# Where TensorE spreads the next pair's delta*u: in front of a pair's expert step, or behind it

## The chip, the cores and the metric

One core of a Trainium2 chip. The metric is the device time of one execution in microseconds.

## The reference

A block of a state-space layer and a mixture of experts over the same 4096 normalised rows x of 256. Cut to what matters:

```python
xn = layernorm(x)
# branch 1: 128 channels d, 64 states n, a scan over the 4096 rows
h = exp(delta[d] * A[d, n]) * h + (delta[d] * u[d]) * B[n]      # each row in turn
y[d] = sum over n of h * C[n]
s = xn + ((y + u * D) * silu(right)) @ W_down
# branch 2: 8 experts, the best 2 for each row
hid = silu(xn @ w1[e]) * (xn @ w3[e]);  out += weight * (hid @ w2[e])
x + s * silu(out)
```

All values are float32.

## The kernel before

**The scan.** The rows are cut into eight chunks of 512. In a chunk the 128 channels form 64 pairs: a pair is two channels with 64 states each on 128 partitions, so there are 512 pairs s, each worked on as 128 x 512. For a pair

- TensorE *spreads* the two channels' delta*u over the states into a PSUM bank: one matmul with a matrix of zeros and ones, `spread(s)`, L1166. Two banks take turns, so a spread waits for the product two before it (L1165).
- VectorE multiplies the spread with B (the *product*, `mult(s)`, L914) and runs the scan (`scan(s)`, L924).
- ScalarE has made the decay, exp(delta * A), into a PSUM bank (L660), from delta that a DMA brought (L565).
- GpSimd multiplies the states by C (`state_by_c`, L420; in the first chunk VectorE does one in four, L960), and TensorE sums the products of four pairs over the states (`reduce_quad`, L1101).

From the second chunk on, every fourth pair (s % 4 == 3) has no spread: GpSimd makes its product from a DMA (L428). So there are 400 spreads.

**The experts.** The chosen rows are sorted by expert into tiles of 256, 39 at most, of which 35 are planned as live. A tile has a turn `rows` (transposes on TensorE, L1138, evicted by ScalarE, L587) and eight turns `step`. In a step TensorE first does the output product of the step three back, `expert_out` (L1123, it needs `hid` from GpSimd, L442), and then `gate_and_up` (L1154) into one of two PSUM banks. ScalarE takes tanh (L595) and a copy (L597) from it, VectorE the *gates* (L936), which frees the bank for the turn after next (`bank_free`, L1169). At a tile's end ScalarE evicts its output (L604). For a tile that is not live TensorE does tiny matmuls instead (L1090).

**The order.** `BY_PAIR` says which turns stand at which pair: steps from pair 64 on, somewhat less than one turn a pair up to pair 484, up to two from there. Among the turns are also the products for the next chunk (L1061) and, at the sixth and eighth pair of a chunk, the two *down* products of the chunk before (`down`, L1110). For these VectorE first closes the chunk in its fifth pair (L943, L945), and then adds each to the rows (`add_rows`, L952), which frees their bank. In pairs 11 to 36 of a chunk VectorE and ScalarE also prepare the next one (a convolution in three taps, L755 and L758; clip, L779). In pairs 0 to 12 of the first chunk TensorE has the up-projections (`left_right`, L1052) and transposes (L1014) of all chunks.

Each engine runs its own queue in the order written. VectorE's, for each pair, cut to what matters here:

```python
            for s in range(PAIR_COUNT):
                if not on_pool(s):
                    mult(s)
                ...
                if s:
                    scan(s - 1)
                    gates(BY_PAIR[s - 1])
                c, at = s // PAIRS, s % PAIRS
                if c and at == 5:
                    gate_chunk(c - 1)
                if c and at - 2 in DOWN_AT:
                    add_rows(c - 1, DOWN_AT[at - 2])
```

TensorE's is in the functions that follow.

Of the kernel before, what the change touches and what calls it, by code (L numbers as in the profile page):

```python
# [14 lines left out]
PAIR_COUNT = NC * PAIRS  # L15
# [67 lines left out]
def on_pool(s):  # L83

    return s >= PAIRS and s % 4 == 3
# [19 lines left out]
def states(s, on_vector):  # L105

    return sum(state_on_vector(i) == on_vector for i in range(s + 1))
# [14 lines left out]
def mamba_and_experts(nc, x, gam, bet, w_up, b_up, conv_w, conv_b, w_dl, b_dl, w_b2, w_c2, a_log,  # L122
                      dvec, w_dn, b_dn, gate, w_all, c_ident, c_upper, c_pick, c_win, c_first,
                      c_start, c_token, out):
    with ExitStack() as ctx:
# [145 lines left out]
        def ge(eng, s, n):  # L271

            if n > 0:
                eng.wait_ge(s, n)
# [733 lines left out]
        def _(pe):  # L1008
# [24 lines left out]
            def transpose_y(c):  # L1033

                pe.wait_ge(s_yh, c + 1)
                if c == 0:
                    pe.wait_ge(s_xev, NC)
                elif c == 1:
                    pe.wait_ge(s_rt, 1)
                else:  # L1040
                    pe.wait_ge(s_lrev, c)
                transpose_chunk(yh, (c % YH_RING) * TC, banks[0:2] if c == 0 else gu_bank).then_inc(s_ytr, 1)

            def left_right(c):

                pe.wait_ge(s_yev, c + 1)
                if c == 1:
                    pe.wait_ge(s_slot, 1)
                ge(pe, s_lrev, c)
                for m, bank in enumerate((banks[2], banks[3]) if c == 0 else (o_bank, gu_bank[0])):  # L1050
                    for h in range(2):
                        ins = pe.matmul(bank[:, :], wup[:, h, m * P:(m + 1) * P], colsT[c % 2][:, h, :],  # L1052
                                        start=(h == 0), stop=(h == 1))
                ins.then_inc(s_lr, 1)

            def product(c, kind):

                if kind == "delta":
                    pe.wait_ge(s_u, c + 1)
                w = wdl[:, :] if kind == "delta" else wbc[:, "bc".index(kind), :]  # L1060
                pe.matmul(product_bank(c, kind)[:, :], w, stage("u"), start=True, stop=True).then_inc(s_dp if kind == "delta" else s_bc, 1)  # L1061
# [30 lines left out]
            def reduce_quad(q):  # L1092

                i = q % QUADS
                pe.wait_ge(s_hc, states(4 * q + 3, False))
                ge(pe, s_hcv, states(4 * q + 3, True))
                if i == 0:
                    pe.wait_ge(s_bcev, 2)
                    ge(pe, s_gt2, q // QUADS)
                for g in range(4):  # L1100
                    ins = pe.matmul(y_bank[32 * g:32 * g + 32, :], win[:, 30 - 2 * i:62 - 2 * i],  # L1101
                                    p_ring[:, (4 * q + g) % P_RING, :], start=(i == 0), stop=(i == QUADS - 1),
                                    skip_group_check=True)
                ins.then_inc(s_red, 1)

            def down(c, h):

                pe.wait_ge(s_gated, c + 1)
                for n in range(2):
                    ins = pe.matmul(bank_of(("down", c, h))[:, n * D:(n + 1) * D], gated[:, (2 * h + n) * P:(2 * h + n + 1) * P],  # L1110
                                    wdn[:, :], start=True, stop=True)
                ins.then_inc(s_dn, 1)

            def expert_out(k):

                i, r = k // KS, k % KS
                pe.wait_ge(s_hid, k + 1)
                if r == 0:
                    ge(pe, s_oev, i)

                def products():
                    for s in range(SH):
                        ins = pe.matmul(o_bank[:, s * D:(s + 1) * D], hid[:, k % 4, s * P:(s + 1) * P],  # L1123
                                        wring[:, r, 4 * P:WROW], start=(r == 0 and s == 0), stop=(r == KS - 1),
                                        skip_group_check=True)
                    return ins

                if_live(i, products, o_bank, s_o)

            def transpose_rows(i):  # L1130

                bank = bank_of(("rows", i, 0))
                pe.wait_ge(s_xg, 32 * (i + 1))

                def products():
                    for h in range(2):
                        for s in range(SH):
                            ins = pe.transpose(bank[:, h * SLOT + s * P:h * SLOT + (s + 1) * P],  # L1138
                                               xg[:, s, h * P:(h + 1) * P], ident[:, :])
                    return ins  # L1140

                if_live(i, products, bank, s_tr)

            def gate_and_up(i, kk):

                bank = bank_of(("step", i, kk))
                if kk == 0:
                    pe.wait_ge(s_xgT, i + 1)
                pe.wait_ge(s_w[kk], 16 * (i + 1))

                def products():
                    for m in range(2):
                        for h in range(2):
                            ins = pe.matmul(bank[:, m * SLOT:(m + 1) * SLOT], wring[:, kk, (2 * m + h) * P:(2 * m + h + 1) * P],  # L1154
                                            xgT[:, i % 2, h, :], start=(h == 0), stop=(h == 1))
                    return ins

                if_live(i, products, bank, s_gu)

            def spread(s):  # L1160

                c, g, i16 = s // PAIRS, s % 4, (s % PAIRS) // 4
                if s % PAIRS == 0:
                    pe.wait_ge(s_stack[c % 2], 32 * (c // 2 + 1))
                ge(pe, s_bm, ORDER[s] - 1)  # L1165
                pe.matmul(du_bank[ORDER[s] % 2][:, :], pick[:, QUADS * (g % 2) + i16, :], stack[:, c % 2, g // 2, :],  # L1166
                          start=True, stop=True).then_inc(s_sel, 1)

            def bank_free(n):  # L1169

                if n < 2:
                    pe.wait_ge(s_lrev, NC)
                    return
                kind, t, k = TURNS[n - 2]
                if kind == "step":
                    pe.wait_ge(s_gt, KS * t + k + 1)
                elif kind == "rows":
                    pe.wait_ge(s_xgT, t + 1)
                elif kind == "down":
                    pe.wait_ge(s_add, 2 * t + k + 1)  # L1180
                elif kind == "delta":
                    pe.wait_ge(s_dlt, KD * t + 1)
                else:
                    pe.wait_ge(s_bcev, 2 * t + 1 + "bc".index(kind))

            def turns(here):

                for turn in here:
                    kind, t, k = turn
                    if kind == "step" and KS * t + k >= LAG:  # L1190
                        expert_out(KS * t + k - LAG)
                    bank_free(NUMBER[turn])
                    if kind == "rows":
                        transpose_rows(t)
                    elif kind == "step":
                        gate_and_up(t, k)
                    elif kind == "down":
                        down(t, k)
                    else:
                        product(t, kind)  # L1200

            spread(0)
            for s in range(PAIR_COUNT):
                if s + 1 < PAIR_COUNT and not on_pool(s + 1):
                    spread(s + 1)
                if s % 2 == 0 and s <= 2 * (NC - 2):
                    left_right(s // 2 + 1)
                if s % 2 == 1 and s <= 2 * (NC - 2) - 1:
                    transpose_y(s // 2 + 2)
                if s % 4 == 3 and s >= 7:  # L1210
                    reduce_quad((s - 7) // 4)
                turns(BY_PAIR[s])
            reduce_quad(PAIR_COUNT // 4 - 1)
            turns(BY_PAIR[PAIR_COUNT])
            for k in range(KS * TILES - LAG, KS * TILES):
# [41 lines left out]
```

## Time and profile before

| | |
|---|---|
| median of three runs | 1525.58 us (1524.34 to 1527.27) |
| the profiled execution's own time | 1526.07 us |
| its span, from the first to the last instruction | 1524.3 us |
| busy TensorE / VectorE / GpSimd / ScalarE | 1222.2 / 1222.3 / 1154.3 / 721.6 us |
| mean granted TensorE clock | 0.900 of full speed |

Three engines are busy for three quarters or four fifths of the span, so the busy times of the whole say little on the bound. The stages differ: set-up until the first scan at 103.5 us, the first chunk without experts up to some 266, the expert steps among the pairs up to 1376, the last pairs with the steps of tiles that are not live, and from 1458 the last sums and stores. Matmul ends in the profile are modelled.

### The profile page before, as it was taken

The numbers are of one execution on the slowest core, as the hardware profiler recorded it, in microseconds if no ns is written. First come the engines' busy times: TensorE is split into PE (matmuls) and PEld (weight loads), VectorE is DVE, ScalarE is ACT, GpSimd is POOL, SyncE is SP. The second block draws the span as 40 slices with busy tenths as digits, with TensorE's granted clock in tenths as the row PEclk, the third lists the DMA queues.
The fourth block names the chain that finished last, engine by engine and source line by source line (L and its number), as shares of the span: only waits on it lengthen the run. The fifth ranks groups of instructions, "written<-read, shape, count | busy, mean of one in ns | idle before, by whom it ended". The sixth has DMA issues, their size and how long they took to land. (4 is left out here: it accounts for less than half of the span.)

```text
span 1524.3 us, 21337 instructions
## 1 busy us (share of the span) xinstructions
PE 1222.2 (80%) x5496; PEld 860.7 (56%) x5496; DVE 1222.3 (80%) x1597; ACT 721.6 (47%) x1557; POOL 1154.3 (76%) x1088
## 2 busy tenths in 40 slices
PE   5737655889988999889989999889988999896720
PEld 5613111566756677556666677657756676674410
DVE  6545999888787978799888987898778988787738
ACT  1445533464544555354555555455535555455611
POOL 0233788779896888778987888789977788799953
PEclk9969655899999999999999999999999999997555
DMA  9843697556564557446655855646744684754336
GB/s 239 168 128 94 169 283 206 150 151 189 172 224 132 171 165 254 129 133 204 220 158 160 250 171 158 228 126 208 232 140 127 181 259 149 255 166 145 121 117 221
DMA packets 173124, 272.52 MB, mean 179 GB/s; under 512 B 28544, under 2 KB 70144, under 8 KB 172992
## 3 DMA queue, kind: packets, MB, share of 16 engines
q10 hardware_dynamic: 111072, 173.93, 39.3%
q1 hardware_dynamic: 55104, 78.41, 16.7%
q0 software_dynamic: 6816, 18.69, 3.2%
q8 instruction: 50, 0.82, 0.2%
q14 instruction: 82, 0.67, 0.1%
HBM read 225.20 MB, written 45.76 MB: 178 GB/s over the span
## 5 line engine op out<-in xcount | busy, mean ns | idle before, releaser
L420 POOL TENSOR_TENSOR arena<-arena,c_rep 128x512 f32<-128x512 f32 x498 | 595.5, 1202 | 183.9 <-DVE arena L924 177.8
L924 DVE TENSOR_TENSOR_SCAN arena<-bank,carry,arena 128x512 f32<-128x512 f32 x512 | 651.9, 1274 | 75.2 <-ACT bank L660 69.9
L1154 PE MATMUL bank<-xgT,wring 128*128 128x256 f32 x2240 | 534.1, 381 | 17.8 <-DVE xn L952 7.1
L660 ACT ACTIVATE bank<-arena,a_neg 128x512 f32<-128x512 f32 x512 | 354.7, 693 | 261.5 <-DVE arena L924 111.0
L1154 PEld LDWEIGHTS bank<-xgT,wring 128*128 128x128 f32 x2240 | 424.0, 190 | 87.7 <-DVE gt L936 13.8
L1123 PE MATMUL bank<-wring,hid 128*128 128x256 f32 x1120 | 301.3, 392 | 44.9 <-ACT o_sb L604 44.6
L914 DVE TENSOR_TENSOR arena<-bank,b_rep 128x512 f32<-128x512 f32 x400 | 272.3, 681 | 40.4 <-PE bank L1166 32.4
L1166 PE MATMUL bank<-stack,pick 128*128 128x512 f32 x400 | 234.7, 598 | 73.3 <-DVE arena L914 51.9
L595 ACT ACTIVATE th<-bank 128x256 f32<-128x256 f32 x312 | 118.9, 381 | 367.6 <-PE bank L1154 309.2
L1123 PEld LDWEIGHTS bank<-wring,hid 128*128 128x128 f32 x1120 | 205.8, 192 | 150.2 <-issue 101.9
L442 POOL TENSOR_TENSOR hid<-gt,ue 128x256 f32<-128x256 f32 x312 | 244.9, 786 | 38.3 <-DVE gt L936 34.9
L936 DVE SCALAR_TENSOR_TENSOR gt<-th,bank 128x256 f32<-128x256 f32 x312 | 126.3, 405 | 132.1 <-ACT th L595 65.9
L1166 PEld LDWEIGHTS bank<-stack,pick 128*128 128x128 f32 x400 | 83.3, 209 | 141.6 <-DVE arena L914 96.3
L1101 PE MATMUL bank<-arena,win 128*32 128x512 f32 x1024 | 157.2, 690 | 3.0 <-POOL arena L420 3.0
L428 POOL TENSOR_TENSOR arena<-arena,b_rep 128x512 f32<-128x512 f32 x112 | 142.6, 1273 | 0.1
L597 ACT ACTIVATE ue<-bank 128x256 f32<-128x256 f32 x312 | 117.7, 377 | 6.9 <-POOL hid L442 6.8
L448 POOL DMA_INDIRECT results<-o_sb,goal x78 | 78.1, 1001 | 26.1 <-issue 16.5
L410 POOL DMA_INDIRECT x_sorted<-xn,route x64 | 64.3, 1005 | 37.9 <-DVE xn L885 24.8
L1090 PEld LDWEIGHTS bank<-ident 128*128 128x128 f32 x136 | 31.0, 293 | 39.6 <-issue 38.1
L1090 PE MATMUL bank<-ident 128*128 128x2 f32 x136 | 30.9, 324 | 24.9 <-POOL hid L442 13.8
L1110 PE MATMUL bank<-wdn,tails 128*128 128x256 f32 x64 | 24.2, 519 | 31.3 <-DVE tails L945 20.6
L1101 PEld LDWEIGHTS bank<-arena,win 128*32 128x32 f32 x1024 | 21.2, 114 | 49.2 <-issue 36.2
(148 smaller groups left out, 744.9 us busy)
## 6 DMA issues: line engine op xcount, KB each, us to landing
arena<-delta_d ACTq DMA_DIRECT2D x512, 256.0 KB, 4.0
arena<-du_d ACTq DMA_DIRECT2D x112, 256.0 KB, 4.2
wring<-in_w_all SPq DMA_DIRECT2D x64, 384.0 KB, 5.5
x_sorted<-arena SPq DMA_DIRECT2D x2, 5031.0 KB, 38.5
xg<-x_sorted ACTq DMA_DIRECT2D x39, 256.0 KB
arena<-results SPq DMA_DIRECT2D x16, 512.0 KB, 6.3
xn<-in_x SPq DMA_DIRECT2D x4, 1024.0 KB, 9.5
parts_d<-spare SPq DMA_DIRECT2D x16, 256.0 KB, 4.2
```

The lines of the kernel that those rows point to most:

```text
L420: pool.tensor_tensor(p_ring[:, s % P_RING, :], h_ring[:, s % H_RING, :], of_chunk(c_rep, c, 2), ALU.mult).then_inc(s_hc, 1)
L428: pool.tensor_tensor(product_with_b(s), product_with_b(s), b_rep[:, cols(c)], ALU.mult).then_inc(s_bp, 1)
L442: pool.tensor_tensor(hid[:, k % 4, :], gt[:, k % 2, :], ue[:, k % 2, :], ALU.mult).then_inc(s_hid, 1)
L595: act.activation(th[:, :], bank[:, 0:SLOT], ACT.Tanh, scale=0.5).then_inc(s_th, 1)
L660: act.activation(a_bank[s % 2][:, :], dl_ring[:, s % D_RING, :], ACT.Exp, scale=a_neg[:, s % PAIRS:s % PAIRS + 1]).then_inc(s_exp, 1)
L914: v.tensor_tensor(product_with_b(s), du_bank[n % 2][:, :], b_rep[:, cols(c)], ALU.mult).then_inc(s_bm, 1)
L924: v.tensor_tensor_scan(out=h_ring[:, s % H_RING, :], data0=a_bank[s % 2][:, :], data1=product_with_b(s), initial=carry[:, q:q + 1], op0=AL ...
L936: v.scalar_tensor_tensor(out=gt[:, k % 2, :], in0=th[:, :], scalar=1.0, in1=bank_of((turn, i, kk))[:, 0:SLOT], op0=ALU.add, op1=ALU.mult). ...
L1101: ins = pe.matmul(y_bank[32 * g:32 * g + 32, :], win[:, 30 - 2 * i:62 - 2 * i], p_ring[:, (4 * q + g) % P_RING, :], start=(i == 0), stop=( ...
L1123: ins = pe.matmul(o_bank[:, s * D:(s + 1) * D], hid[:, k % 4, s * P:(s + 1) * P], wring[:, r, 4 * P:WROW], start=(r == 0 and s == 0), stop ...
L1154: ins = pe.matmul(bank[:, m * SLOT:(m + 1) * SLOT], wring[:, kk, (2 * m + h) * P:(2 * m + h + 1) * P], xgT[:, i % 2, h, :], start=(h == 0) ...
L1166: pe.matmul(du_bank[ORDER[s] % 2][:, :], pick[:, QUADS * (g % 2) + i16, :], stack[:, c % 2, g // 2, :], start=True, stop=True).then_inc(s_ ...
```

## The change

On TensorE the spread of pair s + 1 is issued behind the turns of pair s, not in front of all that pair s has. It also comes behind the up-projection, the transposes and the reduction that pair s may have. The first spread stays where it is.

```diff
             spread(0)
             for s in range(PAIR_COUNT):
-                if s + 1 < PAIR_COUNT and not on_pool(s + 1):
-                    spread(s + 1)
                 if s % 2 == 0 and s <= 2 * (NC - 2):
                     left_right(s // 2 + 1)
                 if s % 2 == 1 and s <= 2 * (NC - 2) - 1:
                     transpose_y(s // 2 + 2)
                 if s % 4 == 3 and s >= 7:
                     reduce_quad((s - 7) // 4)
                 turns(BY_PAIR[s])
+                if s + 1 < PAIR_COUNT and not on_pool(s + 1):
+                    spread(s + 1)
             reduce_quad(PAIR_COUNT // 4 - 1)
```

## Rows read from the trace of the kernel before

**Rows 1.** Busy us by stage: PE, PEld, DVE, ACT, POOL; PEclk, DMA, GB/s

```profile
158.00:266.00 108.00, 60.60 (x150) 16.92 (x149) 102.93 (x118) 41.18 (x71) 85.37 (x83) 0.56 0.82 227
266.00:1376.00 1110.00, 1006.41 (x4748) 736.95 (x4749) 928.09 (x1134) 563.37 (x1246) 925.73 (x883) 0.98 0.59 181
1376.00:1458.00 82.00, 54.15 (x224) 35.21 (x222) 57.32 (x82) 45.37 (x112) 76.08 (x77) 0.58 0.37 117
```

**Rows 2.** TensorE's waits, 270 to 1376 us: us in total, times, longest

```profile
PE bank L1123 <- ACT o_sb L604: 44.6, 33, 2.1
PE bank L1110 <- DVE tails L945: 19.0, 6, 4.2
PE bank L1110 <- DVE xn L952: 10.6, 6, 2.5
PE bank L1154 <- DVE xn L952: 7.1, 6, 1.8
PE bank L1061 <- DVE gt L936: 5.3, 3, 2.4
PE bank L1154 <- DVE spare L779: 4.2, 4, 2.1
PE bank L1154 <- DVE gt L936: 4.0, 6, 1.1
PE bank L1166 <- DVE arena L914: 3.3, 7, 0.8
```

**Rows 3.** VectorE's waits in the same stretch

```profile
DVE gt L936 <- ACT th L595: 65.3, 56, 4.0
...
DVE gt L936 <- ACT ue L597: 48.1, 35, 2.0
```

**Rows 4.** Timeline, pairs 135 to 137: start, length, engine, line, idle

```profile
457.75 1.89 PE L1154 MATMUL bank<-xgT,wring 128*128 128x256 f32 x8
...
459.29 0.58 PE L1166 MATMUL bank<-stack,pick 128*128 128x512 f32 x1
...
460.43 0.42 DVE L936 SCALAR_TENSOR_TENSOR gt<-th,bank 128x256 f32<-128x256 f32 x1 [3.65 <-ACT th L595]
...
461.50 1.13 PE L1110 MATMUL bank<-wdn,tails 128*128 128x256 f32 x4 [1.62 <-DVE xn L952]
...
462.28 0.58 PE L1166 MATMUL bank<-stack,pick 128*128 128x512 f32 x1
...
462.70 1.02 PE L1123 MATMUL bank<-wring,hid 128*128 128x256 f32 x4
```

**Rows 5.** Timeline of VectorE, 704 to 706 us

```profile
704.04 0.66 DVE L914 TENSOR_TENSOR arena<-bank,b_rep 128x512 f32<-128x512 f32 x1
704.63 1.27 DVE L924 TENSOR_TENSOR_SCAN arena<-bank,carry,arena 128x512 f32<-128x512 f32 x1
705.82 0.39 DVE L936 SCALAR_TENSOR_TENSOR gt<-th,bank 128x256 f32<-128x256 f32 x1
```

**Rows 6.** Timeline of VectorE, then of TensorE, at the start of chunk 6

```profile
1120.71 0.42 DVE L936 SCALAR_TENSOR_TENSOR gt<-th,bank 128x256 f32<-128x256 f32 x1 [0.61 <-POOL hid L442]
...
1124.31 2.04 PE L1110 MATMUL bank<-wdn,tails 128*128 128x256 f32 x4 [4.16 <-DVE tails L945]
```

**Rows 7.** Timeline of VectorE, pairs 13 and 14

```profile
152.94 0.69 DVE L914 TENSOR_TENSOR arena<-bank,b_rep 128x512 f32<-128x512 f32 x1
...
154.78 0.73 DVE L758 SCALAR_TENSOR_TENSOR spare<-c_rep,half,spare 128x512 f32<-128x512 f32 x1
156.98 0.69 DVE L914 TENSOR_TENSOR arena<-bank,b_rep 128x512 f32<-128x512 f32 x1 [1.48 <-PE bank L1166]
158.63 1.28 DVE L924 TENSOR_TENSOR_SCAN arena<-bank,carry,arena 128x512 f32<-128x512 f32 x1 [0.96 <-ACT bank L660]
```

**Rows 8.** Busy time in two short stretches, columns as in rows 1

```profile
800.00:803.00 3.00, 3.00 (x11) 2.42 (x10) 2.20 (x3) 0.00 (x0) 3.00 (x4) 0.63 0.57 200
1124.00:1130.00 6.00, 5.69 (x17) 2.91 (x18) 4.91 (x6) 0.69 (x1) 3.20 (x3) 0.51 0.30 101
```

## The prediction

> **What bounds the kernel now.** I read the busy times by stage first [rows 1]. From pair 15 to 62 VectorE is busy 102.93 of 108 us. In the stretch of the expert steps, 1110 us of the span of 1524.3, TensorE is busy 1006.41 us, 91%, against 928.09 on VectorE and 925.73 on GpSimd. In the one behind it, where the last pairs run with the steps of tiles that are not live, GpSimd is busy 76.08 of 82. So most of the time belongs to TensorE, and a change of its order is worth what it does to TensorE's 104 idle microseconds among the expert steps. The view of waits says what ends them [rows 2]: ScalarE's eviction of a tile's output (44.6 us, 33 times), VectorE's closing of a chunk and its two additions to the rows (19.0, 10.6 and 7.1 us, six times each), and gates and clips (5.3, 4.2 and 4.0 us, 13 times). The waits that the change takes aim at, a spread in front of a step that waits for a product on VectorE, come to 3.3 us there. Seen from VectorE, the gates waited for ScalarE's tanh or copy 56 and 35 times [rows 3], 91 of the 280 steps of live tiles: in a third of the steps VectorE is ahead of TensorE, in the others it is late on its own account.
>
> **The change part by part.** The same 400 spreads run, no DMA moves, and no wait is written that was not there. Only TensorE's queue changes; SP's, ScalarE's and GpSimd's keep their order. Between two steps there stands one spread as before, but it is that of the pair whose product VectorE needs next, no longer that of the pair after it.
>
> *What is late next.* VectorE's iteration s+1 is: product of s+1, scan of s, gates of the step of s, all in one queue. Before, the spread of s+1 was done before the step of s, so where VectorE was ahead only the gates were left when the step ended. Now product, scan and gates all stand behind the step. The price of this way from TensorE over VectorE follows from two timelines [rows 4, 5]. A step's gate-and-up matmuls begin at 457.75 and the spread behind them at 459.29: 1.54 us. The spread lasts 0.58, and the product needs it whole. From product to scan are 0.59 (704.04 to 704.63), from scan to gates 1.19 (to 705.82). That makes 1.54 + 0.58 + 0.59 + 1.19 = 3.90 us from the step's begin to its gates. Today it is 460.43 - 457.75 = 2.68. **Such a hop costs 1.22 us more** where VectorE was ahead; where its gates are already that late, it costs nothing.
>
> *Where a hop is paid.* With a step in every pair the gates' lateness is hidden: the step after next needs the bank that they free, and a whole step lies between. It is paid where TensorE today stands idle for VectorE. The gates of pair 135 [rows 4] run at 460.43, the addition to the rows follows, and TensorE, 1.62 us idle, begins the second down product at 461.50. At a chunk's start [rows 6] the gates at 1120.71 are followed by the two operations that close the chunk, and TensorE begins at 1124.31 after 4.16 us idle; what stands behind that down product waits with it, since TensorE keeps its order. These are the three sixes of the waits [rows 2]: the closing, the second down product, and the step that needs the second addition. 18 x 1.22 = 22.0 us. I take off two, for chunk starts at which VectorE is late anyway (a choice): 16 x 1.22 = **+19.5**. Bounds: half of the 18, 11.0, and all, 22.0.
>
> *The 13 waits for gates and clips* are of the same kind, but many lie where VectorE has extra work for the next chunk and is late already. Between 0 and 13 x 1.22 = 15.9 I take a third, **+5.3**, as a third of the gates wait for ScalarE [rows 3].
>
> *The first pairs.* For pairs 1 to 13 the spread now follows a chunk's up-projection or its transposes. The chain of these between TensorE and ScalarE does not wait for it, but VectorE does [rows 7]: the product of pair 13 runs at 152.94; VectorE is through with what follows it, the scan of 12 and a tap of the convolution, at 154.78 + 0.73 = 155.51, 2.57 us later. Behind the projection its spread takes the place that pair 14's has today, so it runs at 156.98, the product of 14 at 159.55 and the scan of 13 0.59 later, at 160.1, where it is at 158.63: **+1.5**. The stage behind it is VectorE's, which carries this on. In that stage almost no pair has a turn, and a spread waited for the product two pairs back in any case: the edit costs nothing, hidden behind VectorE's 95%; were VectorE not the bound there, its reductions would delay the spreads.
>
> *The last pairs.* The spread now stands behind steps that wait for GpSimd. GpSimd's 82 - 76 = 6 idle microseconds are little room. Bounds 0 and one hop for each of the seven groups of four pairs, 8.5; I take **+2**, near the lower end, as an engine that is nearly full hides what others lose.
>
> *The waits for the eviction* end a fixed time after a step, and a spread inside them is free. Every fourth pair has no spread; gone through in the order that the program writes out, 12 of the 33 waits gain one and two lose one. A spread takes at most 462.70 - 462.28 = 0.42 us [rows 4]. Between 0 and 10 x 0.42 = 4.2 I take half, **-2**.
>
> *The clock.* After the 4.16 us idle the granted clock is 0.51 over 6 us, that is, mostly 1.2 GHz, and 0.63 over 3 us after an addition's wait at pair 264 [rows 8], against a mean of 0.98 in the stretch [rows 1]. A fall costs at most 6 x 0.49 = 2.9 or 3 x 0.37 = 1.1 us; I take 2.0. The six waits before the second down product grow from 1.6 to 2.8 us. Between no fall and six, 12 us, I take three, **+6**. The Trainium skill, TensorE: Matmul & The Clock Gate, section "What's actually happening", has the low clock as the engine's default, which activity lifts, and lets it fall after an idle window of its own; read strictly, these six need not fill one, and by that the sum would be 6 us lower. The row at pair 264 speaks for falls.
>
> **Sum.** 19.5 + 5.3 + 1.5 + 2 - 2 + 6 = +32.3 us. The profiled execution took 1526.07 us (span 1524.3, the rest lies around it), so 1558.4; it stands 0.5 above the median of the three runs, which gives **1558 us**.
>
> **The rivals.**
> *A, no change:* VectorE is late at the 18 places anyway, so a hop costs nothing. For it: in two thirds of the steps the gates did not wait for ScalarE. Against: at such a place nothing but the step held them, VectorE had waited 3.65 us for tanh before 460.43 [rows 4]. What is left is 1.5 + 2 - 2, so 1527.
> *B, faster:* TensorE, the bound, loses the 3.3 us in front of the spreads and wins 4.2 at the evictions: 7.5 less, 1518. It decides if a hop costs under 7.5 / 18 = 0.4 us. For it: TensorE's 91%. Against: nothing in the chain [rows 4, 5] can be left out.
> *C, much slower:* all hops at full price, six falls, the last pairs at their upper end: 22.0 + 15.9 + 1.5 + 8.5 + 12 = 60, so 1586, and beyond if GpSimd, which gets its inputs 1.2 us later in a third of the steps, falls behind as well. For it: GpSimd is 83% busy. Against: its product is needed only three steps later.
>
> **How the numbers follow.** The forecast has 0.70, A 0.14, B 0.08, C 0.08. The forecast's own range goes from half of the 18 hops with the first pairs and all of the evictions' gain (11.0 + 1.5 - 4.2 = 8, so 1534) to 1586. A lies below it. To leave out no more than two tenths the range is 1530 to 1584. 0.2%, 3 us, is about what a measurement of this kernel can tell from no change: slower 0.78, same 0.14, faster 0.08.
>
> **What would show it.** In the changed profile VectorE's products wait for their spread in about as many pairs as the gates waited for ScalarE before, and the gates' 113 us of waiting nearly vanish. From a step's first matmul to its gates are 3.9 us where VectorE is ahead. TensorE's waits for the closing and the additions grow from 36.7 us towards 57 at the same counts, some with a lower clock behind them; those for the eviction stay near 45. The scan of pair 13 comes 1.5 us later, and the stage from there to pair 62 is as long as before. I am wrong if the gates do not move against their step, or if they move and those 18 waits do not grow: then the time there was not TensorE's.

## The result, and the profile after

The changed kernel takes **1594.01 us** (median of 4 runs, 1592.76 to 1595.03) against 1526.42 (1524.34 to 1528.68) for the kernel before on the same chip: a ratio of 1.0443, 95% interval 1.0422 to 1.0464, 4.4% slower. The forecast was 1558, in a range of 1530 to 1584: the direction was right, and the loss is 68 us where 32 were forecast.

The same three stages as [rows 1], each moved by what its beginning and its end fell back (the scans of pairs 62 and 484 come 2.1 and 52.0 us later):

```profile
160.10:268.10 108.00, 60.53 (x154) 16.89 (x150) 103.57 (x121) 41.04 (x70) 88.55 (x85) 0.57 0.77 229
268.00:1428.00 1160.00, 1018.42 (x4757) 744.08 (x4750) 925.20 (x1134) 565.49 (x1250) 929.22 (x883) 0.97 0.56 173
1428.00:1526.00 98.00, 55.87 (x214) 35.78 (x213) 57.68 (x82) 44.30 (x108) 76.28 (x77) 0.54 0.31 97
```

About 2 us are lost before pair 62, 50 among the expert steps and 16 in the last pairs; what follows is as long as before. VectorE and GpSimd do the same work in nearly the same busy time. TensorE in the second stage is busy 1018.42 us where [rows 1] has 1006.41, so 12.0 of the 50 are longer busy time for the same instructions, and its idle time rose from 103.6 to 141.6, by 38.0.

TensorE's waits in that stage, beside [rows 2]:

```profile
PE bank L1123 <- ACT o_sb L604: 42.2, 33, 2.0
PE bank L1110 <- DVE tails L945: 24.5, 6, 6.6
PE bank L1110 <- DVE xn L952: 19.6, 7, 2.9
PE bank L1154 <- DVE gt L936: 13.9, 20, 2.1
PE bank L1154 <- DVE xn L952: 12.5, 7, 2.0
PE bank L1154 <- DVE spare L779: 8.0, 5, 4.1
PE bank L1101 <- POOL arena L420: 7.9, 8, 2.6
PE bank L1123 <- POOL hid L442: 3.3, 3, 1.8
PE bank L1061 <- DVE gt L936: 2.6, 2, 2.0
PE bank L1138 <- DVE gt L936: 2.3, 4, 1.2
PE bank L1061 <- DVE spare L765: 2.1, 2, 1.5
```

The closing and the two additions (tails and twice xn) grew from 36.7 to 56.6 us. The waits for gates and for the convolution (gt and spare) went from 14.2 to 28.9. The same view of the kernel before has, below the rows shown of it, what belongs to the two GpSimd rows (and 0.7 us for L765):

```profile
PE bank L1101 <- POOL arena L420: 1.3, 3, 0.7
...
PE bank L1123 <- POOL hid L442: 0.3, 1, 0.3
```

So TensorE waits 9.6 us more for GpSimd, a wait that the forecast did not have. The waits of a spread for a product, 3.3 us, are gone.

VectorE's own waits there, beside [rows 3]:

```profile
DVE arena L914 <- PE bank L1166: 187.7, 142, 4.4
DVE gt L936 <- ACT th L595: 15.6, 12, 2.5
...
DVE gt L936 <- ACT ue L597: 1.2, 3, 0.4
```

The gates wait for ScalarE 15 times instead of 91; the products wait for their spread instead, 142 times.

**One hop.** The timeline of pairs 135 to 137, beside [rows 4]:

```profile
473.53 1.89 PE L1154 MATMUL bank<-xgT,wring 128*128 128x256 f32 x8
475.07 0.58 PE L1166 MATMUL bank<-stack,pick 128*128 128x512 f32 x1
...
475.68 0.69 DVE L914 TENSOR_TENSOR arena<-bank,b_rep 128x512 f32<-128x512 f32 x1 [4.38 <-PE bank L1166]
476.29 1.27 DVE L924 TENSOR_TENSOR_SCAN arena<-bank,carry,arena 128x512 f32<-128x512 f32 x1
477.48 0.39 DVE L936 SCALAR_TENSOR_TENSOR gt<-th,bank 128x256 f32<-128x256 f32 x1
...
477.79 0.68 DVE L952 TENSOR_TENSOR xn<-xn,bank 128x512 f32<-128x512 f32 x1
...
478.53 1.13 PE L1110 MATMUL bank<-wdn,tails 128*128 128x256 f32 x4 [2.88 <-DVE xn L952]
479.31 0.58 PE L1166 MATMUL bank<-stack,pick 128*128 128x512 f32 x1
```

The gates come 477.48 - 473.53 = 3.95 us behind the step's first matmul where it was 2.68, and TensorE idles 2.88 us in front of the second down product where it was 1.62: one hop, 1.26 us. The last row is the next spread: it stands behind the product that itself waited, so VectorE's next product waits too.

**The last pairs.** The view of waits of the whole core, 1428 to 1526 us, and the timeline behind pair 487, the first with two steps:

```profile
DVE arena L914 <- PE bank L1166: 22.2, 13, 4.0
POOL arena L420 <- DVE arena L924: 18.7, 12, 3.8
PE bank L1090 <- DVE gt L936: 18.5, 11, 3.2
```

```profile
1434.89 0.78 PE L1090 MATMUL bank<-ident 128*128 128x2 f32 x4 [3.30 <-ACT o_sb L604]
1435.53 0.60 PE L1166 MATMUL bank<-stack,pick 128*128 128x512 f32 x1
1436.16 0.69 DVE L914 TENSOR_TENSOR arena<-bank,b_rep 128x512 f32<-128x512 f32 x1 [3.95 <-PE bank L1166]
1436.77 1.28 DVE L924 TENSOR_TENSOR_SCAN arena<-bank,carry,arena 128x512 f32<-128x512 f32 x1
1437.96 0.40 DVE L936 SCALAR_TENSOR_TENSOR gt<-th,bank 128x256 f32<-128x256 f32 x1
1438.12 1.26 POOL L420 TENSOR_TENSOR arena<-arena,c_rep 128x512 f32<-128x512 f32 x1 [2.90 <-DVE arena L924]
...
1439.31 0.59 PE L1090 MATMUL bank<-ident 128*128 128x2 f32 x2 [3.18 <-DVE gt L936]
```

The engines stand in turn for each other here: TensorE for ScalarE's eviction, VectorE for the spread, GpSimd for the scan, TensorE for the gates. Before the change, from 1376 to 1458 us, three of these waits were short: products waited for their spread 0.7 us in all, GpSimd for scans 1.6 and TensorE for gates 4.8. GpSimd is busy as long as before (76.28 us, 76.08 in [rows 1]), but in 98 us instead of 82.

**The clock.** Granted clock (third figure from the end) over 4 us, behind the second down product of chunk 5 before, and behind the same product after:

```profile
963.00:967.00 4.00, 3.95 (x18) 3.50 (x19) 3.67 (x4) 0.82 (x2) 2.34 (x3) 1.00 0.47 140
```

```profile
998.00:1002.00 4.00, 3.59 (x9) 2.86 (x10) 1.78 (x3) 0.36 (x2) 1.48 (x2) 0.60 0.23 74
```

TensorE had idled 1.62 us in front of this product before and 2.88 us after. At 1.00 it runs at 2.4 GHz; 0.60 means mostly 1.2 GHz. After the change the clock over such 4 us is 0.57 to 0.63 behind six of the seven second down products in this stage, which follow idles of 2.55 to 2.88 us; behind the one of 478.53 above it stays 1.00. Before, it is 0.59 behind one of them, after an idle of 2.51 us, and 1.00 behind the five with idles of 1.62 or 1.63.

In the whole stage the clock fell 14 times where it had fallen 7 times, and it was at 1.2 GHz for 54.6 us instead of 37.5. At half the clock a busy engine loses half of that time, so the 17.1 us more cost at most 8.5: this is an estimate of the clock's part in the 12.0 us of longer busy time. What the other 3.5 are is not shown.

### The profile page after: what moved, and what is told of

The parts are those of the page before. It is cut to its first block and busy times, and to the rows that moved or that the text cites. A ratio compares the mean times of both kernels' runs of the same rounds, so it can differ in the third digit from the quotient of the medians.

```text
span 1592.7 us, 21337 instructions
## 1 busy us (share of the span) xinstructions
PE 1237.9 (78%) x5496; PEld 869.1 (55%) x5496; DVE 1217.9 (76%) x1597; ACT 722.8 (45%) x1557; POOL 1158.3 (73%) x1088
## 5 line engine op out<-in xcount | busy, mean ns | idle before, releaser
L1154 PE MATMUL bank<-xgT,wring 128*128 128x256 f32 x2240 | 540.7, 385 | 37.0 <-DVE gt L936 13.9
L1123 PE MATMUL bank<-wring,hid 128*128 128x256 f32 x1120 | 303.8, 394 | 45.7 <-ACT o_sb L604 42.2
L1166 PE MATMUL bank<-stack,pick 128*128 128x512 f32 x400 | 230.1, 596 | 67.1 <-DVE arena L914 45.6
```

## The experiments

The runs below were made on four chips. Each is set against runs of the kernel before on its own chip, whose medians were between 1524.5 and 1525.9 us.

### In which pairs the time is lost

One edit makes seven kernels. `late(s)` says in which pairs the spread stands behind the turns; elsewhere it stands in front, as before.

```diff
             for s in range(PAIR_COUNT):
+                if s + 1 < PAIR_COUNT and not on_pool(s + 1) and not late(s):
+                    spread(s + 1)
...
                 turns(BY_PAIR[s])
-                if s + 1 < PAIR_COUNT and not on_pool(s + 1):
+                if s + 1 < PAIR_COUNT and not on_pool(s + 1) and late(s):
                     spread(s + 1)
```

**First pairs, expert steps, last pairs.** `late` is s < 63, 63 <= s < 484, and s >= 484.

> The spread stands behind the turns only up to pair 62, before everywhere else. If the lateness of the first pairs' products is simply carried on by VectorE, as the prediction has it, +1.5 us over the kernel before (about 1528); the trace of the changed kernel has pair 62 2.1 us later. If the up-projections and transposes in front of the spreads cost on TensorE itself, some 5 us or more.

> The spread stands behind the turns only in pairs 63 to 483. The traces of before and after differ by 50 us over these pairs; if the stretches add up, 1526 + 48 to 50 = about 1575. The prediction's terms for them (closing and additions, gates and clips, evictions, clock) had 29, so 1555. If part of the 50 was brought along from the first pairs or is given back in the last ones, clearly less than 1570.

> The spread stands behind the turns only from pair 484 on. The trace of the changed kernel loses 16 us there, where the prediction had 2. If these are a cost of the order in the last pairs alone, +16 (about 1542); if GpSimd, nearly full there before, only paid because it came to them late, under 6.

Measured: 1527.86 us (ratio 1.0022, 1.0008 to 1.0036), 1575.71 (1.0332, 1.0298 to 1.0365) and 1543.63 (1.0130, 1.0094 to 1.0167) against 1525.4. That is +2.5, +50.3 and +18.2, together 71 where the whole change costs 68: the three parts add up, and each is made in its own stage.

**Three pairs of each chunk, and all others among the expert steps.** `late` is s % 64 in (4, 7, 9) for pairs 64 to 483, then the rest of 63 to 483.

> The kernel before, with the spread behind the turns only at the fourth, seventh and ninth pair of chunks 1 to 7 (21 of 512 pairs; these are the pairs whose gates come ahead of the closing and of the two additions). The prediction's term for them was 19.5 us and up to 6 of clock, so 1545 to 1551. If the 18 waits are paid whatever the order, no change.

> The kernel before, with the spread behind the turns in all other pairs from 63 to 483. The prediction gave these 5.3 - 2 = 3 us, so 1529. The 50 us of the whole stretch less 20 to 26 for the 21 places leave 24 to 30: 1550 to 1556. If the two parts use the same waits, each alone costs more than its share and they sum to more than 50.

Measured: 1540.06 us (1.0096, 1.0074 to 1.0118) and 1556.98 (1.0203, 1.0180 to 1.0225) against 1524.8: +15.3, below its range, and +32.2. The forecast's 18 waits hang on the steps of these three pairs (the closing, and the two additions, follow their gates); they make less than a third of the 50. TensorE's waits in the first of the two:

```profile
PE bank L1110 <- DVE tails L945: 18.9, 6, 4.2
PE bank L1110 <- DVE xn L952: 18.2, 7, 2.8
PE bank L1154 <- DVE xn L952: 11.6, 7, 2.0
```

The additions' waits grow by 12.1 us, but the closing's six do not grow at all (19.0 before). With the spread late in all other pairs instead, the closing's waits are 23.7 us. So the late spread in the pair whose gates stand in front of the closing does not by itself make it dearer. At four of the six places the gates come at most 0.2 us later behind their step than before. At the two others they come 1.2 and 1.3 us later, but at one of these the closing's second operation is 1.6 us shorter (0.77 us, 2.40 before; more on it in the last section).

**Pairs 4 to 10 of each chunk, and all others.** Subtracting the two traces, the start of each step's first gate-and-up matmul, shows where TensorE falls back: 35 us in pairs 0 to 12 of the chunks, 6.5 in pairs 13 to 23 and 7 in all 252 others. So the split was made anew.

> The spread stands behind the turns only in pairs 4 to 10 of chunks 1 to 7 (49 pairs), elsewhere in front. Theory (the loss among the expert steps is made where VectorE closes a chunk and adds its rows, and pairs 5, 6, 8 and 10, which the run with pairs 4, 7 and 9 left as they were, share in it): about +38 us, so 1563, as the scans fell back by 38 us in pairs 5 to 10 of the chunks in the changed kernel. Rival (the steps of the other pairs lose through late gates, as the run with all other pairs and its +32 us seemed to say): about +20 us, 1545.

> The complement: the spread stands behind the turns in pairs 63 to 483 except pairs 4 to 10 of chunks 1 to 7. Theory: between +8 and +14 us, 1533 to 1539: what is lost in pairs 24 to 36 and 50 to 63 less what VectorE wins back in pairs 11 to 23. Rival (late gates cost in every pair): about +30 us, 1555. With the run above it should make about 50.

Measured: 1546.82 us (1.0174, 1.0138 to 1.0210) and 1550.21 (1.0177, 1.0157 to 1.0197) against 1524.5. That is +22.3 and +25.7. The theory's numbers did not come out; the rival's, 1545 and 1555, are nearer: about half of the loss is made in each part. The waits of TensorE say what each half is made of. The first:

```profile
PE bank L1110 <- DVE xn L952: 19.6, 7, 2.9
PE bank L1110 <- DVE tails L945: 19.4, 6, 4.8
PE bank L1154 <- DVE xn L952: 12.3, 7, 2.0
```

and the second:

```profile
PE bank L1154 <- DVE gt L936: 12.7, 21, 1.8
PE bank L1154 <- DVE spare L779: 8.0, 5, 4.1
PE bank L1101 <- POOL arena L420: 7.9, 8, 2.6
```

Pairs 4 to 10 pay at both additions, 14.2 of the 14.6 us by which closing and additions grow there (the closing itself hardly grows in this run, 19.0 to 19.4), and by longer busy time: TensorE is busy 1014.23 us in the stage, 7.8 more than before. The other pairs pay in the waits for gates, clips and GpSimd, with a busy time of 1007.75.

### Whether the late spread by itself is the cause

**Gates ahead of the product.** The changed kernel, with scan and gates of the pair before in front of the product in VectorE's queue. Then TensorE's late spread no longer delays them. The same edit in the kernel before makes the opposite mismatch.

```diff
-                if not on_pool(s):
-                    mult(s)
                 if s > 1 and state_on_vector(s - 2):
                     state_by_c(s - 2)
                 if s:
                     scan(s - 1)
                     gates(BY_PAIR[s - 1])
+                if not on_pool(s):
+                    mult(s)
```

> The changed kernel, with VectorE's order in a pair changed too: scan and gates of the pair before first, then the product of this pair. Nothing else. If the time was lost because scan and gates stood in VectorE's queue behind a product that waits for its spread (theory: the hop over VectorE), the gates come 2.7 us after their step's begin again and nearly all is won back: 1525 to 1540. Rival: the loss is TensorE's own, from steps and reductions that now stand in front of spreads, or from GpSimd; then the place of the product on VectorE matters little and it stays above 1575.

> The kernel before, with only VectorE's order changed: scan and gates of the pair before, then the product of this pair. It tells what of the 18 us that stay with both orders changed is the price of VectorE's order itself: then about 1543 here too. If VectorE's order is free by itself (each product is still ahead of its scan by a pair), about 1526, and the 18 us belong to the spread's place.

Measured: 1544.59 us (1.0127, 1.0090 to 1.0163) against 1525.4, so 49 of the 68 are won back, among them the whole loss of the last pairs; and 1597.81 (1.0482, 1.0455 to 1.0508) against 1524.8. The first lies 5 us above the range of its theory: the 19 us that stay are lost among the expert steps, where TensorE is busy 1014.36 us, 8.0 more than in the kernel before, and the closing and additions cost 44.4 us instead of 36.7. The second missed both of its expectations by more than 50 us. In it, TensorE's spreads wait for products that now stand behind the gates:

```profile
PE bank L1166 <- DVE arena L914: 70.9, 56, 2.4
```

With this queue on VectorE a spread behind the step is 53 us faster than one in front; with the kernel's own queue it is 68 us slower. So most of the loss comes from the two orders not matching; with both late, 19 us stay.

**Spread behind the first of two turns.** The changed kernel, but in a pair with two turns the spread stands between them.

```diff
-                turns(BY_PAIR[s])
+                turns(BY_PAIR[s][:1])
                 if s + 1 < PAIR_COUNT and not on_pool(s + 1):
                     spread(s + 1)
+                turns(BY_PAIR[s][1:])
```

> The changed kernel, but where a pair has two turns (eight pairs from 484 on, and no others) the spread stands between them, behind the first. If the last pairs lose their 16 us because product, scan and the first step's gates wait for a spread that stands behind the second step too, most of it comes back: 1576 to 1581. If one step in front of the spread is already enough there, because GpSimd's results come late, it stays at 1590 or above.

Measured: 1583.63 us (1.0390, 1.0363 to 1.0417), with runs from 1576.08 to 1587.98. In its profiled execution, the one of 1576.08, the scans fall back by 3.9 us from pair 484 to 511 where they fall back by 16.3 in the changed kernel. By the medians the edit wins back 10 us; 1583.63 lies between the two expectations. So two steps in front of one spread make the larger part of the 16 us in the last pairs, not all of it.

### Which of VectorE's operations is the late one

**Gates before the scan; then closing and additions before it too.** Both from the changed kernel.

```diff
                 if s:
-                    scan(s - 1)
                     gates(BY_PAIR[s - 1])
+                    scan(s - 1)
```

In the second, the line `scan(s - 1)` stands behind `gate_chunk` and `add_rows`.

> The changed kernel, but VectorE does a pair's gates in front of its scan, so that product and gates alone stand behind the step: 2.7 to 2.8 us from a step's begin to its gates instead of 3.9. The closing of a chunk and the additions keep their places behind the scan. Theory (the closing pairs pay by the chain spread, product, scan, addition, not by the gates alone): the waits for gates, clips and GpSimd fall to about what they were before, the 16 us of the last pairs fall by half or more, the closing and the additions stay: 1560 to 1575. Rival (late gates are all of it): 1530 to 1540.

> As the run before it, but the closing of a chunk and the additions to the rows also stand in front of the scan, so that the scan is the last of VectorE's iteration. Theory: the hop of 1.2 us goes at these places too, some 20 us less than the run before it: 1540 to 1555; what stays is that a spread stands behind a down product that itself waits, so that VectorE waits with it. Rival (the scan, now the late one, delays GpSimd and the sums over the states): no gain or a loss against the run before it.

Measured: 1607.59 us (1.0551, 1.0531 to 1.0570) and 1569.01 (1.0302, 1.0283 to 1.0321) against 1524.5. Both missed their expectations. The first is 14 us slower than the changed kernel, the second 39 faster than the first. The first one's TensorE waits:

```profile
PE bank L1101 <- POOL arena L420: 17.4, 17, 3.0
...
PE bank L1123 <- POOL hid L442: 11.8, 9, 2.1
```

With the scan behind the gates GpSimd gets the states later, and its queue has states and hid in turn; this would make hid late although the gates are early. In the second run the closing and the additions cost 31.4 us, less than the 36.7 before the change, and TensorE wins 6.6 us in pairs 5 to 12 of the chunks where the changed kernel loses 28.0; GpSimd's two waits stay (17.3 and 12.9), and the last pairs lose 23 us. So scan and gates are both awaited, the one by GpSimd, the other by TensorE: neither order is free everywhere.

**Closing and additions before the scan only where they are.** The order is turned in three of a chunk's 64 iterations, in the changed kernel and in the kernel before.

```diff
                 c, at = s // PAIRS, s % PAIRS
+                closing = c and (at == 5 or at - 2 in DOWN_AT)
                 if s:
-                    scan(s - 1)
+                    if not closing:
+                        scan(s - 1)
                     gates(BY_PAIR[s - 1])
...
                     add_rows(c - 1, DOWN_AT[at - 2])
+                if closing:
+                    scan(s - 1)
```

> The changed kernel, but in the three iterations of a chunk in which VectorE closes the chunk before or adds its rows (the sixth, ninth and eleventh pair), it does gates, closing and addition first and the scan behind them; everywhere else the scan stays in front of the gates. Theory (among the expert steps most is lost at the chunk starts, where closing and additions stand a product and a scan behind a late spread): the 28 us that TensorE's steps lose in pairs 5 to 12 of the chunks fall by 20 to 30, the rest stays as in the changed kernel: 1564 to 1574. Rival (GpSimd's inputs come late wherever the scan is put behind the gates, which made the run with gates before every scan slower): under 10 us won, 1585 or more.

> The kernel before, with the same three iterations turned round. Theory: with the spread in front, product and scan are mostly done while VectorE waits for the step's tanh, so the closing and the additions come hardly earlier: within 6 us of the kernel before, rather faster, 1519 to 1526. Rival (product and scan delay them as much as in the changed kernel): 20 us faster or more.

> The kernel before, with gates, closing, scan in that order in the sixth pair's iteration of a chunk only; the additions keep their places. Theory (the gain of 21 us came from the closing, whose six waits fell from 19.0 to 7.6 us while those for the additions stayed at 17 to 18): 15 to 21 us faster than before, 1505 to 1511. Rival (all three iterations share in it): about a third, 7 us.

Measured: 1561.1 us (1.0227, 1.0202 to 1.0252); 1504.83 (0.9863, 0.9838 to 0.9887) against 1525.5; and with the closing's iteration alone turned, in the kernel before, 1510.93 (0.9897, 0.9879 to 0.9914) against 1525.9. The changed kernel wins 33 us: closing and additions fall from 56.6 to 32.8 us of waits, and TensorE's busy time from 1018.42 to 1005.00. The kernel before wins 21, as the rival had it and not the theory, 15 of them by the closing alone. Its closing waits, 19.0 before:

```profile
PE bank L1114 <- DVE tails L945: 7.6, 6, 2.5
```

### Whether GpSimd's lateness costs by itself

**The sums over the states one pair later**, except in the first nine pairs of a chunk, in the changed kernel and in the kernel before; then both edits that helped the kernel before together.

```diff
+                put_off = lambda s: PAIRS <= s < MOE_LIVE and s % PAIRS > 8
+                if s % 4 == 0 and put_off(s - 1):
+                    reduce_quad((s - 8) // 4)
-                if s % 4 == 3 and s >= 7:
+                if s % 4 == 3 and s >= 7 and not put_off(s):
                     reduce_quad((s - 7) // 4)
```

> The changed kernel, with the sums over the states (TensorE's reductions) one pair later in the pairs of the expert steps, except in the first nine pairs of a chunk. Theory (late gates make GpSimd late, and TensorE then stands at a reduction): the 7.9 us in 8 waits of reductions for GpSimd vanish and the time falls by 4 to 10 us, to 1584 to 1590. Rival (GpSimd's lateness costs nothing by itself, the wait goes to the next place): within 3 us of the changed kernel.

> The kernel before with the same later reductions, to set the run before it against. Its reductions wait for GpSimd 3 times and 1.3 us in all: within 3 us of the kernel before by either theory, unless the later reductions delay GpSimd, whose ring of products they free: then slower by more.

> The kernel before with both edits that made it faster by themselves: the scan behind the closing and the additions in three iterations of a chunk (21 us), and the sums over the states one pair later outside the first nine pairs of a chunk (4 us). If they add up: 1500 to 1502. If the later sums only take waits that the other edit has taken already: 1504 to 1506.

Measured: 1589.59 us (1.0422, 1.0391 to 1.0453), 1521.04 (0.9968, 0.9956 to 0.9981), 1505.76 (0.9858, 0.9835 to 0.9882). The edit wins 4 us by the medians in either kernel. In the kernel before this is clear of the noise; in the changed kernel the intervals overlap (1.0391 to 1.0453, and 1.0422 to 1.0464 without the edit). So nothing shows a win that belongs to the change. In the changed kernel the reductions' waits for GpSimd fall from 7.9 to 3.5 us, but the steps' waits for gates rise from 13.9 to 25.3. Here the wait goes on to the next place, as the rival had it, though the median lies in the theory's range. On top of the turned scan the later sums win nothing measurable: 1505.76 against 1504.83 of that edit alone. **The fastest kernel of this study is the one before with the scan behind closing and additions, 1504.83 us**, 1.4% below the kernel before.

## Why the forecast had the direction and not the size

**What held.** The hop held as forecast: gates 3.95 us behind their step's begin (3.90 forecast), the gates' 113 us of waiting down to 17, products waiting for spreads instead (in 142 pairs, where about 91 were forecast), the eviction's waits near 45 (42.2, a gain of 2.4 where 2 was forecast), and the first pairs 2 to 2.5 us (1.5).

**What came out partly by luck.** The closing and additions grew from 36.7 to 56.6 us, **+19.9 where +19.5 was forecast**. At the second down product the hop is there: five waits grow from 1.62 or 1.63 to 2.88 us. But the counts were to stay, and there are 20 waits instead of 18, the two new ones with 3.0 us. The closing's +5.5 us is not the hop forecast for it, since it does not grow when only these three pairs have the late spread.

**What failed.** The failing step is "With a step in every pair the gates' lateness is hidden: the step after next needs the bank that they free, and a whole step lies between", with what hangs on it. Its cover is there in most pairs: TensorE falls back only 7 us in 252 of them. It lacks in three places. Of the 36 us that the forecast is short, 14 lie in the first of these, 9.4 in the second and 9.6 in the third; 6 are longer busy time. Against these stand 3.3 us of waits for products, which went away and were not counted.

- *Last pairs: +16 to 18, forecast +2.* Up to two steps stand in a pair, and the spread behind both, so the step after next stands right behind the spread instead of a pair later. "An engine that is nearly full hides what others lose" was the wrong end of the bounds, which themselves (0 to 8.5) were too low: they priced one hop per four pairs, and a loop of TensorE, VectorE and GpSimd lies there. GpSimd did not hide the lateness: it waited 18.7 us for scans where it had waited 1.6, and these 17 us are the size of the loss. The runs that kept the gates ahead of the product, or put the spread behind the first turn, took all or most of this loss away.
- *Pairs in which VectorE has extra work: +14.7 of waits for gates and clips, forecast +5.3.* I argued that VectorE is late there already, so that a hop costs little. The rows say the reverse: before the change all 14.2 us of these waits lie in pairs 11 to 36 of the chunks, where VectorE prepares the next one, and after it 26.7 of the 28.9. That little of the cover is left there because VectorE is late is my reading; no run takes the extra work away.
- *GpSimd: +9.6 of waits, forecast nothing* ("its product is needed only three steps later"). Later scans make later states, and its queue has states and hid in turn. That this wait costs time by itself is not shown: the later sums took part of it away and the waits for gates rose.

**The clock** term was too small: the busy time grew by 12.0 us, of which the clock has 8.5 by the estimate above, where 6 was taken. Three falls behind the second down products were forecast, and six came. The Trainium skill, TensorE: Matmul & The Clock Gate, section "What's actually happening", was read in the forecast so that idles of 2.8 us need not lower the clock. The six falls behind idles of 2.55 to 2.88 us decide against that reading.

**The sum among the expert steps** then is 19.9 + 14.7 + 9.6 - 2.4 - 3.3 and 1.0 of other waits = 39.5 us of waits, where the stage's idle time grew by 38.0. With 12.0 of longer busy time that is 50.0 by the windows, where 28.8 were forecast (19.5 + 5.3 - 2 + 6). With 2 and 16 us of the other stages that is the 68. Rival C, 1586, had nearly the size for nearly these reasons (all hops, six falls, last pairs at their upper end, GpSimd behind) and 0.08 of the chances.

**Rivals A and B** fall with the time, and with the additions' waits: there the hop was not free. But A was right for most of the closings: at four of these six places the gates come hardly later in the run with three pairs changed. In the kernel before, its time was not set by the step's gates alone: moving the scan behind it won 15 us, and the last section shows that its second operation itself was slowed.

**What stays open:** how the 22 and 26 us of the two halves divide further, what the closing's +5.5 us come from, and what the 19 us are that stay when both orders are late. Each half alone makes waits that the other shares (the closing grows by 0.4 and 2.9 us in them, by 5.5 in the whole change), and a wait removed at one place came back at the next in the run with later sums.

## What to carry to other kernels

Where two in-order engines feed each other twice per round, price a moved instruction by the whole loop that it closes (here spread, product, scan, gates, step), and look for where the loop has less slack: rounds with two steps, rounds in which the other engine has extra work, and consumers of the late engine's other results. A hop at a place where the waiting is visible is only the part that the trace of before can show. When an order on one engine is changed, try the matching order on the other one as well: the scan put behind the closing, three times per chunk, won 21 us in the kernel before, where the change took aim at 3.3 us of waits.

## What the runs showed of the hardware that was not expected

The second operation of the closing (L945), whose two inputs both lie in SBUF, is held by GpSimd. VectorE in the kernel before, and GpSimd at the same time (chunk 3):

```profile
617.67 0.66 DVE L943 TENSOR_TENSOR tails<-bank,tails 128x512 f32<-128x512 f32 x1
...
618.37 3.49 DVE L945 TENSOR_TENSOR tails<-tails 128x512 f32<-128x512 f32 x1
```

```profile
618.15 0.72 POOL L442 TENSOR_TENSOR hid<-gt,ue 128x256 f32<-128x256 f32 x1
618.83 1.25 POOL L420 TENSOR_TENSOR arena<-arena,c_rep 128x512 f32<-128x512 f32 x1
620.05 1.25 POOL L428 TENSOR_TENSOR arena<-arena,b_rep 128x512 f32<-128x512 f32 x1
```

The operation in front of it, of the same shape but with one input in PSUM, takes 0.66 us beside the same GpSimd; L945 takes 3.49 and ends 0.56 us after the last of three GpSimd instructions that followed on each other. In each of the seven closings among the expert steps of the kernel before it ends 0.55 or 0.56 us after a GpSimd instruction that ran beside it. The same group over the whole kernel, before and with the scan behind the closing:

```profile
L945 DVE TENSOR_TENSOR tails<-tails 128x512 f32<-128x512 f32 x8 | 15.2, 1902 | 0.3
```

```profile
L945 DVE TENSOR_TENSOR tails<-tails 128x512 f32<-128x512 f32 x8 | 6.6, 824 | 0.3
```

With the scan behind the closing, six of the eight take 0.69 or 0.70 us, and in five of these no GpSimd instruction overlaps. VectorE is 8.6 us shorter there. At the six closings for which TensorE waits, L945 takes 12.03 us in all before and 5.20 with the scan behind it. So of the 11.4 us by which these six waits fall, 6.8 are this operation being shorter, and 4.6 are left for the scan no longer standing in front. The rest of the 21 us is mostly busy time: TensorE's among the expert steps falls from 1006.41 to 996.87 us, with 3 falls of the clock instead of 7.

The Trainium skill, SBUF — State Buffer, section "Who interferes with whom", says that a VectorE instruction with two SBUF inputs contends with a GpSimd instruction that reads SBUF, and that issue order decides who blocks. The rows agree with the first. They go beyond the second: L945 begins at 618.37, before the GpSimd instructions of 618.83 and 620.05, and ends behind both.
